# An attention kernel with a relative bias: one mix burst of eight key tiles instead of two of four, and one PSUM copy on ScalarE instead of VectorE

## The reference

```python
q, k, v = einsum('bsx,xMnd->Mbnsd', x, qkv)            # 16 heads of 64
a = einsum('bnsd,bntd->bnst', q, k) * 64 ** -0.5
cum = cumsum(rpe_bias, axis=-1)                        # 256 distances per head
bias = where(rel >= 0, cum[:, clip(rel, 0)], -30000.)  # rel = query - key, causal
mix = einsum('bnst,bntd->bnsd', softmax(a + bias), v)
x = layernorm(x + einsum('bnsd,ndx->bsx', mix, out_w))
prev = x shifted by one token
r = sigmoid((mu_r * x + (1 - mu_r) * prev) @ W_r.T)
k = (mu_k * x + (1 - mu_k) * prev) @ W_k.T
out = layernorm(x + r * (square(relu(k)) @ W_v.T))
```

## Time and profile before

| what | value |
|---|---|
| median of three runs | 1164.18 us |
| the profiled execution's own time | 1157.7 us |
| its span | 1156.0 us |
| mean granted TensorE clock | 0.99 |
| PE busy | 1106.1 us (96%) |
| DVE busy | 809.3 us (70%) |
| ACT busy | 731.1 us (63%) |
| a tile step, from one far mix to the next (606.11 to 640.11) | 34.00 us |
| a plain step, likewise (160.07 to 192.27) | 32.20 us |

### The profile page before, as it was taken

The page is one execution under the profiler, slowest core; times in us unless marked ns, Lnnn a source line. Parts: engine busy times, 40 slices in busy tenths (PEclk is TensorE's granted clock), DMA queues, the critical chain, the costliest instruction groups (busy, mean ns, idle before and its releaser), DMA issues.

```text
span 1156.0 us, 21563 instructions
## 1 busy us (share of the span) xinstructions
PE 1106.1 (96%) x6973; PEld 791.9 (69%) x6973; DVE 809.3 (70%) x2121; ACT 731.1 (63%) x1857; POOL 6.4 (1%) x15
## 2 busy tenths in 40 slices
PE   6899999999999999999999999999999999999994
PEld 3666666766677777676777676777666777767773
DVE  2666666666657777776778777778776778777756
ACT  3666667665656676675766676767666667667633
POOL 1000000000000000000000000000000000000000
PEclk9999999999999999999999999999999999999998
DMA  8856565675657666656577656676756666665710
GB/s 200 222 142 150 140 153 145 152 186 137 155 135 168 160 166 161 169 144 174 134 176 171 166 149 155 163 177 164 185 135 155 164 169 158 169 164 144 234 40 20
DMA packets 113005, 180.71 MB, mean 156 GB/s; under 512 B 13152, under 2 KB 69360, under 8 KB 112896
## 3 DMA queue, kind: packets, MB, share of 16 engines
q1 hardware_dynamic: 110736, 178.42, 62.1%
q10 hardware_dynamic: 2160, 0.92, 0.3%
HBM read 58.41 MB, written 20.22 MB: 68 GB/s over the span
## 4 chain that ended last, share of the span: by engine, by line
PE 84%; DVE 5%; DMA 4%; issue 3%; ACT 2%; SPq 2%; POOL 0%; DVEq 0%; ACTq 0%
PE ps_o L1018 22%; PE ps_rows L977 21%; PE ps_t L994 17%; PE ps_m L952 9%; PE ps_m L957 5%; PE ps_m L1034 4%; PE ps_o L994 3%; DMA stacks<-k_lo 2%; DVE pt L684 2%; PE ps_rows L1090 1%; SPq L300 1%; DVE prob L660 1%; DMA prob<-in_L_attn_x 1%; ACT pt L519 1%; DVE mix_sb L691 1%
## 5 line engine op out<-in xcount | busy, mean ns | idle before, releaser
L501 ACT ACTIVATE prob<-prob,low 128x128 f32<-128x128 f32 (+7 forms) x512 | 394.5, 772 | 111.9 <-DVE low L660 106.0
L660 DVE CUSTOM_DVE_ANT_0 prob<-ps_rows,table 128x128 f32<-128x128 f32 (+7 forms) x512 | 379.9, 750 | 52.8 <-PE ps_rows L977 33.9
L977 PE MATMUL ps_rows<-stacks 128*128 128x512 f32 (+3 forms) x1536 | 401.1, 372 | 10.7 <-DMA stacks<-k_lo 6.1
L994 PE MATMUL ps_t<-ident,prob 128*128 128x128 f32 x1984 | 311.4, 278 | 6.4 <-ACT pt L519 3.5
L994 PEld LDWEIGHTS ps_t<-ident,prob 128*128 128x128 f32 x1984 | 231.4, 141 | 90.3 <-issue 74.6
L1018 PE MATMUL ps_o<-pt,v_pair 128*64 128x512 f32 (+3 forms) x1536 | 270.1, 494 | 0.0
L977 PEld LDWEIGHTS ps_rows<-stacks 128*128 128x128 f32 x1536 | 246.1, 190 | 32.0 <-DMA stacks<-k_lo 7.0
L684 DVE COPY pt<-ps_t 128x256 f32<-128x256 f32 (+2 forms) x320 | 178.2, 565 | 124.8 <-PE ps_t L994 124.2
L1018 PEld LDWEIGHTS ps_o<-pt,v_pair 128*64 128x64 f32 x1536 | 102.2, 137 | 177.5 <-issue 165.2
L519 ACT ACTIVATE pt<-ps_t 128x512 f32<-128x512 f32 (+3 forms) x352 | 162.8, 463 | 95.9 <-PE ps_t L994 95.6
L952 PE MATMUL ps_m<-x_cur,w_cur 128*128 128x512 f32 x250 | 131.6, 608 | 5.2 <-DVE q_lo L646 2.0
(11 more groups left out here) (118 smaller groups left out, 607.2 us busy)
## 6 DMA issues: line engine op xcount, KB each, us to landing
stacks<-k_hi SPq DMA_DIRECT2D x126, 256.0 KB, 4.6
stacks<-k_lo SPq DMA_DIRECT2D x126, 256.0 KB, 5.1
inv_all<-inverse_sums SPq DMA_DIRECT2D x128, 128.0 KB, 3.3
stacks<-q_hi SPq DMA_DIRECT2D x63, 256.0 KB, 4.0
stacks<-q_lo SPq DMA_DIRECT2D x63, 256.0 KB, 4.3
mix_transposed<-mix_sb SPq DMA_DIRECT2D x62, 256.0 KB, 3.8
table<-bias_by_distance SPq DMA_DIRECT2D x64, 192.0 KB, 3.6
mix_tile<-mix_transposed SPq DMA_DIRECT2D x24, 512.0 KB, 4.7
```

The source lines that it names most:

```text
L501: nc.scalar.activation(row, row, ACT.Exp, bias=low[:, r:r + 1], scale=-1.0, accum_out=total[:, r:r + 1]).then_inc(s_exp, 1)
L660: nc.vector.tensor_tensor_reduce(prob[:, r % PSLOTS, 0:width], ps_rows[:, score_at(r):score_at(r) + width], table[n % 2][:, h, 0:width][:, ...
L977: ins = nc.tensor.matmul(ps_rows[:, at + c0:at + c1], q_st(h, n)[:, P * i:P * i + P], k_st(h, n, low_part)[:, c0:c1], start=(low_part == 0 ...
L994: ins = nc.tensor.transpose(t_bank[TBANK[k]][:, P * b:P * b + P], prob[:, r % PSLOTS, at:at + P], ident[:, :])
```

## The change

The far mix is done whole in slot 2, where its first four key tiles were before; nothing of it is left in slot 5. DVE's `store_mix` for it moves from slot 6 to slot 3. Bank 10, the first four blocks of row 9 (the tenth slot), is copied by ACT instead of DVE.

```diff
-EVACUATOR = "010110010100011001110111"
+EVACUATOR = "010110010110011001110111"
...
-MIX_FAR = (2, 5)
+MIX_FAR = 2
...
-                    if prev and slot == MIX_FAR[1] + 1:
+                    if prev and slot == MIX_FAR + 1:
                         store_mix(n - 1, 1)
...
-                    if prev and slot in MIX_FAR:
-                        at = GROUP * MIX_FAR.index(slot)
-                        mix(n - 1, 1, at, at + GROUP)
+                    if prev and slot == MIX_FAR:
+                        mix(n - 1, 1, 0, TILES)
```

## The result

| | before | with the change |
|---|---|---|
| median | 1160.02 us (4 runs) | 1189.64 us (4 runs) |
| profiled execution, its span | 1157.7, 1156.0 us | 1188.28, 1186.5 us |
| tile step, plain step | 34.00, 32.20 us | 35.19, 32.76 us |

The account below looks back on a forecast made before the run. PE was taken to set the time, with DVE as critical up to row 14's score; 19.8 us (tile steps) and 4.4 (plain) gave +24.2 on 1157.7, 1181.9, plus 6.5 to the median: 1188.4 us, range 1166 to 1200 (8 in 10).

Parts of the forecast that it names:

- The saving of the switches: PE's far mix: one burst in place of two saves 0.24 us of PE per step, 7.4 us in 31 steps.
- Tile steps, 0.9 us: Steps 9 to 30: PE's score of row 14 comes later with DVE's bias of row 12; 22 x 0.9 = 19.8 us.
- DVE's part of the reckoning: Tile step: DVE ends the bias of row 12 at 624.1 to 624.3, 0.7 to 0.9 us later than before.
- the wait that I put at the score of row 13: Tile step: most of PE's wait of 1.0 to 1.1 us falls ahead of the scores of rows 11 and 13.
- The waits for `low`: PE waits for DVE's `low` ahead of the scores of rows 11 and 13, 20 to 30 us in total.
- Plain steps, 0.55 us: Steps 1 to 8: DVE ends the bias of row 12 later, 0.55 us each; 8 x 0.55 = 4.4 us.
- The store in slot 3, nothing: DVE's store of the mix in slot 3: broadcast sums come in time, nothing waits for it within the step; no cost.
- The copy of bank 10, nothing: Bank 10's copy on ACT, ready before slot 10's transposes: nothing, up to 0.3 us per step as the bad end.
- The ACT rival: Copy of bank 10 on ACT holds up slot 10's transposes by 0.3 us per step, 9 us more: 1197; chance 0.12.
- Step 31, nothing: Step 31 has no projections and about 2 us less work for DVE, so no loss there.
- A PE that never waits: Rival: DVE's lag stays within what PE can bridge; 10 us faster, 1154; chance 0.07.
- a small lag: Rival: waits before row 14 partly made up for; 0.2 to 0.3 us per step, +6 to +9 us, about 1172; chance 0.20.

Follow-up runs that it names:

- store late: The whole change, but the store of the mix stays in slot 6 instead of slot 3; ratio to before 1.0222, tile step 34.70 us.

## Why the prediction was right, point by point

**The bound and the saving.** PE sets the time, and DVE's stretch up to slot 9 is equally tight: bank 6 on ACT shows it. The saving of the switches was 0.24 us and is seen as 0.23.

**Tile steps, 0.9 us: measured 1.19.** DVE's part of the reckoning, 0.7 to 0.9 us, was right: 0.88. What failed is the sentence that PE's score of row 14 moves with DVE's bias of row 12. The score came 0.38 us later than that bias allowed, because PE had been held in slot 8 by ACT's copy of bank 7. I had followed ACT only as far as the high part of slot 7, and bank 7 stands right behind it in its list. In the same way the wait that I put at the score of row 13 is in the transposes of slot 8. The waits for `low` were forecast at 20 to 30 us, and are 10.4, all at row 11; the 26.8 us for ACT's copy were not forecast. The mis-sized term is 22 x 0.9 = 19.8 us, with a measured 26.2.

**Plain steps, 0.55 us: measured 0.56,** and the mechanism holds: the score of row 14 follows DVE's bias of row 12 by 0.05 us, which is 0.57 later than before. That ACT's copy of bank 7, which the reckoning lacks, ends at almost the same point is luck.

**The store in slot 3, nothing.** It never waited for the broadcast sums. But its place is part of the loss, 0.49 us of a tile step (store late), and for tile steps the prediction counted nothing for it, since the store is in DVE's stretch before and after. Of this, 0.17 is in DVE's own stretch; the rest comes through the bias of row 10 and ACT. The sentence that the store to memory keeps its place in SP's list was right with the change. That the place matters showed only when the store was moved later.

**The copy of bank 10, nothing:** shown (0.9985), but for one wait of 0.45 us in step 31. The ACT rival named this copy; what came late on ACT was bank 7's.

**Step 31, nothing: measured 1.1 us,** with a wait of 0.46 us for the bias of row 9 in slot 7 as in the others. To have fewer projections did not spare it.

**The sum.** +24.2 us were forecast, and the profiled executions differ by 30.6. The forecast of 1188.4 us came as near to 1189.64 as it did by luck. It added 6.5 us for the distance between the profiled execution and the median of before; with one more run that distance is 2.3 us, and with the change it is 1.4. This made up for most of the 6.4 us missing in the sum.

**The rivals.** A PE that never waits and a small lag are refuted by the two waits in every undisturbed tile step. The reserve that the small lag asked for is there, though: PE made up for 0.17 us (0.11 in slots 8 and 9, 0.06 in slots 5 and 6), too little against 0.88.

## What to carry to other kernels

An engine's share of busy time doesn't say whether it has room where work is moved to. Take the stretch between two points where the engines meet, subtract only the idle times that the change really removes, and follow every engine's list to the last thing that somebody waits for, not to the first. A burst of the bounding engine is also time that the others use to catch up: work could be moved out of it here up to all the idle time that they had in the stretch behind it (1.44 us, not the 0.99 of the nearest idle time), and was paid for beyond that. If an operation is moved on one engine, look also at the queue that waits for it: whatever stands behind that wait moves too.

## What the runs showed of the hardware that was not expected

A recorded wait of PE costs more than it shows. From the transposes of slot 5 to the score of row 11 the wait of 0.45 us made the stretch 0.64 longer (2.09 against 1.45 us, 697.84 to 699.93 and 616.61 to 618.06): 0.70 for the wait, less the 0.06 that PE made up for. And a mean busy share of 96%, at a granted clock of 1.00 in the tile step, hid 0.14 us of pauses in each tile step that appeared in no list of waits; only the run with bank 6 on ACT brought them out. PE's recorded busy time fell with them, by 6.8 us for the same matmuls (1106.1 to 1099.3), so it is not a measure of work.
